# Cross attention: which batch of a tile takes the key weights' products, and which engine copies U

## The chip, the cores and the metric

The kernel runs on one core of a Trainium2 chip. The metric is the time of one execution in microseconds of device time; a run's number is a median over executions. The core has five engines with queues of their own: TensorE (PE in the profile; PEld are its weight loads), VectorE (DVE), ScalarE (ACT), GpSimd (POOL) and SyncE (SP, which issues the DMAs here). They meet only at semaphores: an instruction adds to a count when it has finished, and another engine waits until the count has reached a value.

## What is computed

A block of three parts over 2048 tokens of width 512: cross attention, self attention with a mask by pages, and a layer of eight experts of which each token uses two. Only the cross attention is touched:

```python
x = x + _L0_xattn_ref(_layernorm(x, axis=-1), ctx_512, Wq, Wkv, Wo)

def _L0_xattn_ref(x, z, Wq, Wkv, Wo):        # x: 64 x 32 x 512, z: 64 x 257 x 256
    Q = (x @ Wq.T).reshape(B, xN, 16, 32)
    KV = (z @ Wkv.T).reshape(B, zN, 2, 16, 32)
    K, V = KV[:, :, 0], KV[:, :, 1]
    attn = softmax(einsum('bqhd,bkhd->bhqk', Q, K) * 32 ** -0.5)
    O = einsum('bhqk,bkhd->bqhd', attn, V).reshape(B, xN, 512)
    return O @ Wo.T
```

There are 64 batches of 32 tokens, each with its own 257 keys.

## The kernel before

A tile is 128 tokens, that is four batches of 32 (BT = 4, j = 0 to 3, called first to fourth batch here); there are 16 tiles, taken in pairs (u = 0, 1), the first and the last pair written out and those between in a loop. The keys are never formed. Q of a tile is multiplied with the key weights once (`absorb_k`, the key products QK, 256 numbers for each of 16 heads and 128 tokens), and the scores of a batch are QK times the batch's z (`scores`). In the same way the weighted sum of z is taken first (`gather_z`, result U), and U of a tile's four batches is multiplied with the value weights at once (`values`). Products of 32-bit numbers are split into a high and a low half and three products (`product`, lines 52 to 54).

Each engine runs its own order for a batch s = 4i + j, written out by hand in a function `tile`:

- TensorE: the scores of s; in the first batch `turn_last` of the tile before; `gather_z` of s - 1; in the first batch `last_values`; in the third the transposition of the normalised x (`turn_x`, line 363); the transposition of the next z (`turn_z`, line 357); a step, if the batch has one; then in the first batch `values` of the tile before (line 436), in the second `project_o` of the tile before, in the third and fourth one half of `project_q` each for tile i + 2 (line 371); and last the transposition of the weights, `turn_p` (line 389).
- A step is two calls of `absorb_k` (line 381, 32 small products each pair). It needs the score banks, so it waits until all exponentials of the batch are done (a_E); ScalarE then copies two times 128x1024 numbers to QK (`qk_out`, line 528, semaphore a_QK), and `turn_p`, which uses two of the same banks, waits for that.
- ScalarE: four exponentials (line 573), in the first batch the copy of U of the tile's last batch before (`u_out`, line 549), the high half of QK for the next batch (`qk_hi`, line 535), in the third batch the copy of the turned x (`x_out`, line 518), the high half of z (line 514), the copies of a step, in the other batches `u_out`, in the first the high half of O, the high half of the transposed weights (line 541), and in the third and fourth batch half of Q (`q_out`, line 523).
- VectorE: the maxima of the scores (line 664), the reciprocal and the normalisation of the weights (line 676), the low half of QK (`qk_lo`, line 608), the low half of z (`z_lo`, line 603), and the low half of the transposed weights (line 616).

Which batch has a step, for which tile, and what it waits for comes from one function, `step_of`, which returns the slot of Q and QK, the first of the two products, the count of a_Q and the count of a_QK. Before, the second batch has the second pair of the next tile, and the fourth batch the first pair of the tile after the next. So two products of tile 1 are made before the tiles begin (AHEAD = 6), and TensorE waits for them there. U's copies count on a semaphore `a_U`, for which `gather_z` and `values` wait.

Of the kernel before, what the change touches and what calls it, by code (L numbers as in the profile page):

```python
# [84 lines left out]
def cross_attention(nc, x_in, ctx_in, Wq, Wkv, Wo, x_res, ident, vlast_dram, spare,  # L85
# [8 lines left out]
    NQ = C // P  # L94
    HD = 32
# [11 lines left out]
    with ExitStack() as ctx:  # L107
# [3 lines left out]
        def sem(name):  # L111
            return ctx.enter_context(nc.semaphore(name))
# [180 lines left out]
        pe_PL, pe_O, pe_Q, pe_OP = (sem(n) for n in ("pe_PL", "pe_O", "pe_Q", "pe_OP"))  # L293
        a_T, a_E, a_PT, a_U, a_QK, a_QKh = (sem(n) for n in ("a_T", "a_E", "a_PT", "a_U", "a_QK", "a_QKh"))
        a_X, a_Q, a_OT = (sem(n) for n in ("a_X", "a_Q", "a_OT"))
# [4 lines left out]
        s_end = BT * n_tile  # L300
        AHEAD = 6

# [8 lines left out]
        def step_of(i, u, j, more):  # L311

            if j == 1 and (more or u == 0):
                return 1 - u, 2, 2 * (i + 1) + 2, BT * i + AHEAD + 2
            if j == 3 and more:
                return u, 0, 2 * (i + 2) + 1, BT * i + AHEAD + 4
            return None

        with nc.Block() as block:
# [28 lines left out]
            def _(pe):  # L350
# [14 lines left out]

                def project_q(i, half):
                    if half == 0:
                        pe.wait_ge(a_X, i + 1)
                    for m in range(2 * half, 2 * half + 2):
                        for k in range(KC):  # L370
                            mm = pe.matmul(bank_o[:, m * P:(m + 1) * P], WqT[:, k, m * P:(m + 1) * P], xnT[:, k, :],
                                           start=(k == 0), stop=(k == KC - 1))
                    mm.then_inc(pe_Q, 1)
# [36 lines left out]
                def gather_z(s):  # L410

                    pe.wait_ge(g_Z, s + 1)
                    pe.wait_ge(v_PT, 2 * s + 2)
                    need(pe, a_U, s)
                    for k in range(KL):
                        for c in range(CH):
                            mm = product(pe, bank_u[:, k],
                                         (zn_hi[:, c, k * P:(k + 1) * P], zn_lo[:, c, k * P:(k + 1) * P]),
                                         (PT_hi[:, c, :], PT_lo[:, c, :]), c == 0, c == CH - 1)
                    mm.then_inc(pe_U, 1)  # L420
# [8 lines left out]
                def values(i):  # L429

                    pe.wait_ge(a_U, BT * i + BT)
                    for m in range(NQ):
                        for part in range(KL):
                            for hh in range(4):
                                h = 4 * m + hh
                                mm = pe.matmul(bank_o[hh * HD:(hh + 1) * HD, m * P:(m + 1) * P],
                                               WvT[:, part, h * HD:(h + 1) * HD], U[:, part, h, :], start=False,
                                               stop=(m == NQ - 1 and part == KL - 1), tile_position=(0, hh * HD))
                    mm.then_inc(pe_O, 1)
# [10 lines left out]
                project_q(0, 0)  # L450
                project_q(0, 1)
                turn_z(0, 0, 0)
# [5 lines left out]
                project_q(1, 0)  # L458
                project_q(1, 1)
                pe.wait_ge(a_QK, NQ)  # L460
                pe.wait_ge(a_Q, 4)
                absorb_k(Qp[1], 0)
                absorb_k(Qp[1], 1)
                pe.wait_ge(a_QK, AHEAD)

# [45 lines left out]
            def _(act):  # L511
# [35 lines left out]
                def u_out(s, j):  # L547
                    act.wait_ge(pe_U, s + 1)
                    act.copy(U[:, :, :, j * HD:(j + 1) * HD], bank_u[:].rearrange("p k (h q) -> p k h q", q=HD)
                             ).then_inc(a_U, 1)  # L550

# [7 lines left out]
                q_out(1, 1, (0, 1))  # L559
                qk_out(NQ, 1, 0)  # L560
                qk_out(NQ + 1, 1, 1)

                def tile(i, u, first, last, more):
                    for j in range(BT):
                        s = BT * i + j
                        some = not (first and j == 0)
                        step = step_of(i, u, j, more)
                        for m in range(NQ):
                            act.wait_ge(v_mx, 2 * s + m // 2 + 1)
                            if m == 0:  # L570
# [3 lines left out]
                                           scale=1.0, accum_out=rsum[:, m:m + 1]).then_inc(a_E, 1)  # L574
                        if j == 0 and some:
                            u_out(s - 1, BT - 1)
                        if not (last and j == BT - 1):
# [22 lines left out]
            def _(dve):  # L600
# [26 lines left out]
                def last_weights(i):  # L627
# [12 lines left out]
                                      head_mask[:].unsqueeze(1).unsqueeze(3).to_broadcast(heads), ALU.mult).then_inc(v_PR, 1)  # L640

                def ot_lo(i):
                    dve.wait_ge(a_OT, i + 1)
# [13 lines left out]
                def tile(i, u, first, last, more):  # L657
                    for j in range(BT):
# [14 lines left out]
                        if j == 0:  # L673
                            need(dve, v_PR, 4 * i)
                        dve.tensor_tensor(p_last[:, j, :], Pr[:, :, LAST], rinv[:], ALU.mult)
                        dve.tensor_tensor(Pr[:, :, 0:LAST], Pr[:, :, 0:LAST],
                                          rinv[:].unsqueeze(2).to_broadcast([P, NQ, LAST]), ALU.mult).then_inc(v_N, 1)
                        if not (last and j == BT - 1):
                            qk_lo(s + 1, u if j < BT - 1 else 1 - u, (j + 1) % BT)
                            z_lo(s + 1)  # L680
# [1568 lines left out]
```

## Time and profile before

| what | value |
|---|---|
| median of 3 runs | 1547.85 us (1547.23 to 1549.03) |
| the profiled execution's own time | 1552.86 us |
| its span, first to last instruction | 1551.1 us |
| mean granted clock of TensorE over the span | 0.974 |
| busy over the span: TensorE, VectorE, ScalarE, GpSimd | 94%, 69%, 53%, 35% |
| ScalarE's copy of U, 64 times | 1.03 us each (median) |
| ScalarE's copies to QK, 64 times | 1.02 us each (median) |

The profiled execution is 5.0 us longer than the median of the runs shown. Shares over the whole span mix three stages: the cross attention runs from about 22 to 714 us, then self attention, then the experts.

### The profile page before, as it was taken

Reading aid. Unit: us, or ns where it says so; the run is one execution under the profiler, and the core shown is the slowest. Engines: PE = TensorE matmul, PEld = TensorE weight load, DVE = VectorE, ACT = ScalarE, POOL = GpSimd, SP = SyncE. Lnnn points to the kernel's source line nnn. Section 1 sums busy time; section 2 is a strip of 40 time slices with the busy share of each in tenths; the row PEclk is TensorE's granted clock in tenths of the full one; section 3 lists DMA queues with packets and bytes.
Section 4 is the critical chain, followed back from the end, with each engine's and each line's share of the span. In section 5 each row is a group of like instructions: output and inputs, shape, how many; then the busy total and the mean of one; then the engine's idle time right before and its main releaser. Section 6 shows DMA issues by size and latency. Waiting matters only on the chain. (4 is left out here: it accounts for less than half of the span.)

```text
span 1551.1 us, 39390 instructions
## 1 busy us (share of the span) xinstructions
PE 1457.1 (94%) x14912; PEld 1295.2 (84%) x14912; DVE 1064.6 (69%) x1920; ACT 825.1 (53%) x1542; POOL 545.2 (35%) x816
## 2 busy tenths in 40 slices
PE   5799999999999999997899998679999999999997
PEld 5788888888888888885687876579999999999996
DVE  2466666666666676673567676687878878787874
ACT  3566666666666666663334342154554555555552
POOL 1122221222222222222856777343343332334332
PEclk8899999999999999997999999789999999999999
DMA  8101001001010001100010114147877778787871
GB/s 277 64 29 29 29 21 27 25 23 27 27 27 27 21 27 27 29 8 1 16 42 31 37 37 152 57 154 266 278 271 265 267 234 292 251 273 246 291 242 41
DMA packets 130733, 174.10 MB, mean 112 GB/s; under 512 B 16953, under 2 KB 89337, under 8 KB 130626
## 3 DMA queue, kind: packets, MB, share of 16 engines
q1 hardware_dynamic: 120242, 145.56, 28.9%
q0 software_dynamic: 10384, 27.05, 4.8%
q8 instruction: 74, 1.21, 0.3%
q14 instruction: 33, 0.27, 0.1%
HBM read 157.18 MB, written 19.06 MB: 114 GB/s over the span
## 5 line engine op out<-in xcount | busy, mean ns | idle before, releaser
L2046 DVE TENSOR_TENSOR lo<-raw,hi 128x1024 fp32r<-128x1024 f32 x207 | 246.1, 1220 | 7.8 <-ACT hi L1982 6.6
L52 PE MATMUL mo_bank<-xT_hi,hi 128*128 128x256 f32 x768 | 216.6, 282 | 3.2 <-DVE xT_lo L2055 2.8
L54 PE MATMUL mo_bank<-xT_lo,hi 128*128 128x256 f32 x768 | 215.5, 281 | 0.0
L53 PE MATMUL mo_bank<-xT_hi,lo 128*128 128x256 f32 x768 | 215.3, 280 | 0.0
L1982 ACT CAST hi<-raw 128x1024 fp32r<-128x1024 f32 x207 | 208.3, 1049 | 4.9 <-DMA raw<-in_L_ffn_W_dram 2.7
L573 ACT ACTIVATE Pr<-xa_s,nmax 128x257 f32<-128x257 f32 x256 | 119.0, 472 | 130.5 <-DVE nmax L664 130.4
L2002 ACT ACTIVATE sl<-mo_bank 128x256 f32<-128x256 f32 x117 | 44.9, 384 | 247.6 <-PE mo_bank L54 244.7
L52 PE MATMUL xa_s<-zT_hi,QK_hi 128*128 128x258 f32 x512 | 153.6, 300 | 4.0 <-ACT QK L528 2.0
L616 DVE TENSOR_TENSOR PT_lo<-xa_s,PT_hi 128x512 fp32r<-128x512 f32 x128 | 82.4, 685 | 105.9 <-ACT PT_hi L541 105.8
L52 PEld LDWEIGHTS mo_bank<-xT_hi,hi 128*128 128x128 f32 x768 | 145.2, 189 | 9.8 <-issue 5.6
L53 PEld LDWEIGHTS mo_bank<-xT_hi,lo 128*128 128x128 f32 x768 | 145.1, 189 | 3.2
L54 PE MATMUL xa_s<-zT_lo,QK_hi 128*128 128x258 f32 x512 | 146.2, 286 | 0.0
L53 PE MATMUL xa_s<-zT_hi,QK_lo 128*128 128x258 f32 x512 | 145.3, 284 | 0.0
L54 PEld LDWEIGHTS mo_bank<-xT_lo,hi 128*128 128x128 f32 x768 | 145.2, 189 | 0.0
L2130 POOL TENSOR_TENSOR e_carrier<-count 128x1 f32<-128x1 f32 x84 | 29.9, 356 | 313.2 <-DMA of_row<-slot_val 104.9
L664 DVE TENSOR_REDUCE nmax<-xa_s 128x2 f32<-128x514 f32 x128 | 88.1, 691 | 42.6 <-PE xa_s L54 40.9
L707 POOL TENSOR_TENSOR xa_carrier<-mhalf 128x1 f32<-128x1 f32 x64 | 12.6, 197 | 291.7 <-DVE QK_lo L608 287.2
L52 PE MATMUL xa_u<-PT_hi,zn_hi 128*128 128x512 f32 x256 | 103.2, 403 | 0.0
L52 PEld LDWEIGHTS xa_s<-zT_hi,QK_hi 128*128 128x128 f32 x512 | 98.0, 191 | 6.0 <-DVE zT_lo L603 2.8
L53 PE MATMUL xa_u<-PT_hi,zn_lo 128*128 128x512 f32 x256 | 101.9, 398 | 0.0
L54 PE MATMUL xa_u<-PT_lo,zn_hi 128*128 128x512 f32 x256 | 101.8, 398 | 0.0
L52 PE MATMUL mo_bank<-hi,a_hi 128*128 128x512 f32 x234 | 95.8, 409 | 5.3 <-DVE a_lo L2111 5.2
(302 smaller groups left out, 3925.5 us busy)
## 6 DMA issues: line engine op xcount, KB each, us to landing
raw<-in_L_ffn_W_dram SPq DMA_DIRECT2D x207, 512.0 KB
raw<-in_ctx_dram SPq DMA_DIRECT2D x64, 256.0 KB, 2.6
out_dram<-x_res SPq DMA_DIRECT2D x16, 256.0 KB
xs<-xn SPq DMA_DIRECT2D x16, 256.0 KB
x_res<-in_x_dram SPq DMA_DIRECT2D x1, 3840.0 KB, 18.9
VL<-v_last_rows SPq DMA_DIRECT2D x128, 2.0 KB, 1.5
raw_o<-in_L_xattn_Wo_dram SPq DMA_DIRECT2D x1, 1024.0 KB, 5.7
raw_q<-in_L_xattn_Wq_dram SPq DMA_DIRECT2D x1, 1024.0 KB, 8.8
```

Source lines behind the costliest of these rows:

```text
L52: pe.matmul(out, lh, rh, start=start, stop=False)
L53: pe.matmul(out, ll, rh, start=False, stop=False)
L54: return pe.matmul(out, lh, rl, start=False, stop=stop)
L573: act.activation(Pr[:, m, 0:NK], bank_s[:, m, 0:NK], ACT.Exp, bias=nmax[:, m:m + 1], scale=1.0, accum_out=rsum[:, m:m + 1]).then_inc(a_E, 1)
L616: dve.tensor_tensor(PT_lo[:, c, :], bank_pt[c], PT_hi[:, c, :].bitcast(F32), ALU.subtract).then_inc(v_PT, 1)
L664: dve.tensor_reduce(nmax[:, 2 * h:2 * h + 2], bank_s[:, 2 * h:2 * h + 2, 0:NK], AX_X, ALU.max, negate=True).then_inc(v_mx, 1)
L707: pool.tensor_tensor(carrier[:], mhalf[:], mhalf[:], ALU.add)
L1982: aW.done(act.copy(hi, raw), f"p{c}{q}")
L2002: aM.done(act.activation(sl[:, j % 2, :], bank_hg[j % 2][:, 0:ROWS], ACT.Silu), f"{pos}s{j}")
L2046: vW.done(dve.tensor_tensor(lo, raw, hi.bitcast(F32), ALU.subtract), f"p{c}{q}")
L2130: pool.tensor_tensor(carrier[:], count[:, 0:1], count[:, 0:1], ALU.add).then_inc(carried, 1)
```

## The change

Both pairs of the next tile's key products are made in the tile: the first pair in the first batch, the second in the third batch, instead of in the fourth batch of the tile two before and the second of the tile before. So nothing of tile 1 is made ahead of the tiles any more, and both pairs of tile 15 are made in tile 14. `project_q` waits for the copy of the turned x in both halves, and in the second half also for the copy of the first half of Q. The copy of U of a tile's last batch, which is made in the next tile's first batch, goes from ScalarE (behind the exponentials) to VectorE (behind the normalisation of the weights, ahead of `qk_lo`). The semaphore `a_U` is renamed `U_out`, since two engines count on it. The copy of U behind the last tile stays on ScalarE.

```diff
-            if j == 1 and (more or u == 0):
-                return 1 - u, 2, 2 * (i + 1) + 2, BT * i + AHEAD + 2
-            if j == 3 and more:
-                return u, 0, 2 * (i + 2) + 1, BT * i + AHEAD + 4
+            if j % 2 == 0 and (more or u == 0):
+                return 1 - u, j, 2 * (i + 1) + 2, BT * i + NQ + j + 2
             return None
...
-                def project_q(i, half):
-                    if half == 0:
-                        pe.wait_ge(a_X, i + 1)
+                def project_q(i, half, wait_first=True):
+                    pe.wait_ge(a_X, i + 1)
+                    if half == 1 and wait_first:
+                        pe.wait_ge(a_Q, 2 * i + 1)
...
                 pe.wait_ge(a_QK, NQ)
-                pe.wait_ge(a_Q, 4)
-                absorb_k(Qp[1], 0)
-                absorb_k(Qp[1], 1)
-                pe.wait_ge(a_QK, AHEAD)
...
                 q_out(1, 1, (0, 1))
-                qk_out(NQ, 1, 0)
-                qk_out(NQ + 1, 1, 1)
...
-                        if j == 0 and some:
-                            u_out(s - 1, BT - 1)
...
+                def u_out(s, j):
+                    dve.wait_ge(pe_U, s + 1)
+                    dve.tensor_copy(U[:, :, :, j * HD:(j + 1) * HD], bank_u[:].rearrange("p k (h q) -> p k h q", q=HD)
+                                    ).then_inc(U_out, 1)
...
                         dve.tensor_tensor(Pr[:, :, 0:LAST], Pr[:, :, 0:LAST],
                                           rinv[:].unsqueeze(2).to_broadcast([P, NQ, LAST]), ALU.mult).then_inc(v_N, 1)
+                        if j == 0 and not first:
+                            u_out(s - 1, BT - 1)
                         if not (last and j == BT - 1):
                             qk_lo(s + 1, u if j < BT - 1 else 1 - u, (j + 1) % BT)
                             z_lo(s + 1)
```

## Rows read from the trace of the kernel before

**Rows 1.** Busy time per engine, one tile: stretch, its length, engines, PEclk, DMA share, GB/s

```profile
307.00:348.00 41.00, 40.50 (x372) 35.92 (x371) 27.48 (x50) 27.41 (x60) 9.90 (x21) 1.00 0.09 26
```

**Rows 2.** Waits of TensorE's weight loads, 90 to 700 us: total, times, longest

```profile
PEld xa_o L436 <- ACT U L549: 6.5, 15, 0.4
PEld xa_o L371 <- ACT xg L518: 6.2, 13, 0.5
...
PEld xa_s L389 <- ACT QK L528: 3.4, 13, 0.3
```

**Rows 3.** Timeline, a first batch: start, duration, engine, line, operation, idle before

```profile
341.56 1.22 DVE L676 TENSOR_TENSOR Pr<-Pr,rinv 128x1024 f32<-128x1024 f32 x1
...
342.60 0.60 PE L357 MATMUL xa_z<-ident,raw 128*128 128x128 f32 x4
...
343.40 1.95 PE L436 MATMUL xa_o<-U,WvT 128*32 128x128 f32 x64 [0.20 <-ACT U L549]
...
345.29 1.09 PE L389 MATMUL xa_s<-ident,Pr 128*128 128x128 f32 x8
...
346.21 0.39 PE L52 MATMUL xa_s<-zT_hi,QK_hi 128*128 128x258 f32 x1
```

**Rows 4.** Timeline, a second batch

```profile
310.69 0.60 PE L357 MATMUL xa_z<-ident,raw 128*128 128x128 f32 x4
...
312.32 0.50 PE L52 MATMUL xa_o<-WoT_hi,OT_hi 128*128 128x512 f32 x1
...
316.02 0.37 PE L52 MATMUL xa_s<-zT_hi,QK_hi 128*128 128x258 f32 x1
```

**Rows 5.** Timeline, a third batch

```profile
321.81 0.60 PE L363 MATMUL xa_o<-ident,xg 128*128 128x128 f32 x4
...
322.25 0.60 PE L357 MATMUL xa_z<-ident,raw 128*128 128x128 f32 x4
...
323.09 2.05 PE L371 MATMUL xa_o<-xg,WqT 128*128 128x128 f32 x16 [0.24 <-ACT xg L518]
...
325.77 0.36 PE L52 MATMUL xa_s<-zT_hi,QK_hi 128*128 128x258 f32 x1
```

**Rows 6.** Timeline, a fourth batch

```profile
331.54 0.60 PE L357 MATMUL xa_z<-ident,raw 128*128 128x128 f32 x4
...
332.07 1.17 PE L381 MATMUL xa_s<-raw,Wk 32*128 32x128 f32 x32
...
333.18 2.05 PE L371 MATMUL xa_o<-xg,WqT 128*128 128x128 f32 x16
...
336.14 0.36 PE L52 MATMUL xa_s<-zT_hi,QK_hi 128*128 128x258 f32 x1
```

**Rows 7.** Timeline, the beginning and tile 0

```profile
41.33 0.28 PE L371 MATMUL xa_o<-xg,WqT 128*128 128x128 f32 x1
...
45.65 0.39 PE L52 MATMUL xa_s<-zT_hi,QK_hi 128*128 128x258 f32 x1 [2.04 <-ACT QK L528]
...
51.89 0.20 ACT L573 ACTIVATION_READ_ACCUMULATOR Pr<-xa_s,nmax 128x1 f32 x1
...
55.43 0.58 PE L52 MATMUL xa_s<-zT_hi,QK_hi 128*128 128x258 f32 x1
...
61.84 0.60 PE L357 MATMUL xa_z<-ident,raw 128*128 128x128 f32 x4
...
66.49 0.37 PE L52 MATMUL xa_s<-zT_hi,QK_hi 128*128 128x258 f32 x1
```

**Rows 8.** Timeline, third batch of tile 14

```profile
652.35 0.60 PE L357 MATMUL xa_z<-ident,raw 128*128 128x128 f32 x4
...
654.83 0.39 PE L52 MATMUL xa_s<-zT_hi,QK_hi 128*128 128x258 f32 x1 [0.64 <-DVE zT_lo L603]
```

**Rows 9.** VectorE's groups by line over the span: busy, mean ns, idle before

```profile
L603 DVE TENSOR_TENSOR zT_lo<-xa_z,zT_hi 128x512 fp32r<-128x512 f32 x64 | 43.9, 686 | 2.9 <-ACT zT_hi L514 2.9
```

**Rows 10.** Busy time per engine, first scores of tile 0, columns as in rows 1

```profile
45.65:50.20 4.55, 4.55 (x25) 4.55 (x26) 0.69 (x1) 1.02 (x4) 0.00 (x0) 0.62 0.00 0
```

More of the change, by code:

```diff
@@ L293, in cross_attention @@
         pe_PL, pe_O, pe_Q, pe_OP = (sem(n) for n in ("pe_PL", "pe_O", "pe_Q", "pe_OP"))
-        a_T, a_E, a_PT, a_U, a_QK, a_QKh = (sem(n) for n in ("a_T", "a_E", "a_PT", "a_U", "a_QK", "a_QKh"))
+        a_T, a_E, a_PT, a_QK, a_QKh, U_out = (sem(n) for n in ("a_T", "a_E", "a_PT", "a_QK", "a_QKh", "U_out"))
         a_X, a_Q, a_OT = (sem(n) for n in ("a_X", "a_Q", "a_OT"))
@@ L300, in cross_attention @@
         s_end = BT * n_tile
-        AHEAD = 6
         def by_pair(eng, tile):
@@ L413, in gather_z @@
                     pe.wait_ge(v_PT, 2 * s + 2)
-                    need(pe, a_U, s)
+                    need(pe, U_out, s)
                     for k in range(KL):
@@ L429, in values @@
                 def values(i):
-                    pe.wait_ge(a_U, BT * i + BT)
+                    pe.wait_ge(U_out, BT * i + BT)
                     for m in range(NQ):
@@ L450, in _ @@
                 project_q(0, 0)
-                project_q(0, 1)
+                project_q(0, 1, False)
                 turn_z(0, 0, 0)
@@ L458, in _ @@
                 project_q(1, 0)
-                project_q(1, 1)
+                project_q(1, 1, False)
                 pe.wait_ge(a_QK, NQ)
-                pe.wait_ge(a_Q, 4)
-                absorb_k(Qp[1], 0)
-                absorb_k(Qp[1], 1)
-                pe.wait_ge(a_QK, AHEAD)
                 def tile(i, u, first, last, more):
@@ L549, in u_out @@
                     act.copy(U[:, :, :, j * HD:(j + 1) * HD], bank_u[:].rearrange("p k (h q) -> p k h q", q=HD)
-                             ).then_inc(a_U, 1)
+                             ).then_inc(U_out, 1)
                 x_out(0)
@@ L565, in tile @@
                         s = BT * i + j
-                        some = not (first and j == 0)
                         step = step_of(i, u, j, more)
@@ L640, in last_weights @@
                                       head_mask[:].unsqueeze(1).unsqueeze(3).to_broadcast(heads), ALU.mult).then_inc(v_PR, 1)
+                def u_out(s, j):
+                    dve.wait_ge(pe_U, s + 1)
+                    dve.tensor_copy(U[:, :, :, j * HD:(j + 1) * HD], bank_u[:].rearrange("p k (h q) -> p k h q", q=HD)
+                                    ).then_inc(U_out, 1)
                 def ot_lo(i):
```

## The prediction

> **What bounds the kernel now.** I first read the busy time per engine over one tile of the middle of the cross attention: in 41.00 us TensorE is busy for 40.50 us at a granted clock of 1.00, while VectorE and ScalarE are busy for about 27.4 us each [rows 1]. So in this stage the time is TensorE's, and a change is worth what it takes out of TensorE's order or puts into it. Then I read whom TensorE waited for from 90 to 700 us [rows 2]: 6.5 us in 15 waits for ScalarE's copy of U, 6.2 us in 13 waits for the copy of the turned x, 3.4 us in 13 waits for the copies of the key products QK. All three are waits that the change moves. Last I read the timeline of one tile, batch by batch [rows 3 to 6], and the two ends of the stage [rows 7, 8], because the change is not symmetric there. DMA is no part of it: the tile moves its data at a DMA share of 0.09 [rows 1].
>
> I measure a batch by one stretch: from the first transposition of the next z (call it T) to the first score product of the next batch (S). What lies ahead of T, scores and gathering of z, the change leaves alone. T to S is now
>
> - first batch: 346.21 - 342.60 = 3.61 us [rows 3],
> - second: 316.02 - 310.69 = 5.33 us [rows 4],
> - third: 325.77 - 322.25 = 3.52 us [rows 5],
> - fourth: 336.14 - 331.54 = 4.60 us [rows 6],
>
> in sum 17.06 us of the tile.
>
> **Key products moved to the first and third batch.** TensorE's instructions stay the same in number: two absorptions per step, 32 small products, two steps a tile. ScalarE's copies of them move along; no DMA moves.
>
> The fourth batch loses its step. T is followed by 0.44 us of transposes, read from two runs of four behind each other (322.25 - 321.81) [rows 5]. Then comes the projection, and from its start to S without a wait for QK the third batch shows 325.77 - 323.09 = 2.68 us [rows 5]. New: 0.44 + 2.68 = 3.12 us, 1.48 less. Its projection newly waits for ScalarE's copy of the first half of Q; that copy stands right behind the third batch's copies of the transposed weights, so it is done a batch earlier, and I cost the wait at nothing.
>
> The second batch loses its step too. Its output projection starts 312.32 - 310.69 = 1.63 us after T [rows 4], without the step after 0.44: 1.19 less, 4.14 us new. Can the chain follow? At a batch without any step (the third of tile 14) S waits for the low half of z, and T to S is 654.83 - 652.35 = 2.48 us [rows 8]. That is the floor of the chain, and 3.12 and 4.14 lie above it, so TensorE's work still sets both.
>
> The third batch gets a step. Now it has T, projection, transposition of the weights; new it has T, step, projection, transposition, which is what the fourth batch does now, its wait for the QK copies included: 4.60 us, 1.08 more. The wait for the turned x (6.2 us in 13) goes, since the step lies in front of the projection: 1.64 us from T to the projection [rows 6] against 0.84 now [rows 5]. ScalarE has one copy more to do here than in the fourth batch, but it does it before the step's products have ended.
>
> The first batch gets a step as well, ahead of the values' products. These take 1.95 us [rows 3], the projection in the fourth batch 2.05 [rows 6], so the same form fits: 4.60 us, 0.99 more. Queued behind TensorE's wait for QK is the transposition of the weights; on ScalarE the copies (ahead of the copies of O and of the weights) end about when the values' products end, so these two follow with the gap to TensorE that they have now. If the QK wait cost nothing here, 0.15 would be saved; if the values begin late, up to 0.44, today's wait, is added.
>
> Sum for a tile: 0.99 - 1.19 + 1.08 - 1.48 = -0.60 us, with bounds of -0.75 and -0.16. Thirteen tiles (1 to 13) have this form: -7.8 us, from -9.8 to -2.1.
>
> **U copied by VectorE.** VectorE copies after it has normalised the weights. That operation starts at 341.56 and takes 1.22 us [rows 3], so it ends 0.18 us after T. The values start 1.64 us after T, so a copy of up to 1.46 us costs nothing. The trace has no copy of 128x1024 from this memory on VectorE. The nearest rows are the same number of elements in SBUF, 1.22 us [rows 3], and twice the 128x512 subtraction that reads PSUM, 2 x 0.686 = 1.37 us [rows 9]. I take 1.25 as an estimate, nearer to the row with as many elements in one operation; both ends are under 1.46. Behind it on VectorE stand the low halves of QK and of z (1.22 and 0.686 us), which then end about 3.4 us after T, and S is due at 4.60. ScalarE is rid of about as long a copy and reaches its own QK copy earlier. The cover is the step; where there is none, in tile 15, the values now start 0.80 us after T (343.40 - 342.60, [rows 3], since tile 15 has the same first batch) and will start at 0.18 + 1.25 = 1.43 plus a little: 0.6 us more, bounds 0.6 and 0.8.
>
> The Trainium skill (Perfetto Trace Analysis, Optimizing Scalar/DVE Operations) speaks against this move: it gives VectorE a fixed cost of about 125 ns at an access to PSUM and ScalarE about 51 ns. With the 0.96 GHz that the Trainium skill gives (VectorE: DVE Perf Modes, Specifications), an estimate from these two pages for the copy is 1024/0.96 + 125 = 1.19 us; by that the last tile would lose 0.06 us less, and nothing else of the sum would change. No run here shows such a copy yet.
>
> **The ends.** In the beginning, TensorE now waits before its first scores for Q, absorbs two pairs of tile 1 and waits for their copies: scores start at 45.65, while the projection before them has its last product at 41.33 [rows 7]. New they start at about 41.6: 4.05 us earlier. Tile 0 then takes the step in its first batch, with little to cover it. There the exponentials end at 52.09, 6.44 us after the first scores, and from a step's start to S the fourth batch shows 336.14 - 332.07 = 4.07 us [rows 6]: 10.5 us in place of 55.43 - 45.65 = 9.78 [rows 7], 0.7 more. The clock is open here: the scores ran at a granted clock of 0.62 [rows 10] after a stretch in which TensorE mostly waited. If they run at 1.00, 4.55 us of them become 4.55 x 0.62 = 2.8, and 0.7 more becomes 1.0 less; if the transposition of the weights (1.09 us, [rows 3]) falls to half clock, it takes twice that, and it is 1.8 more. In the second batch the step goes and there is no output projection yet: T to S was 66.49 - 61.84 = 4.65 [rows 7] and falls to the floor of 2.48, 2.17 less. Third and fourth batch as in every tile: +1.08 and -1.48. Tile 0: -4.05 + 0.7 - 2.17 + 1.08 - 1.48 = -5.9 us, from -7.6 to -4.8.
>
> In tile 14 the first and second batch give +0.99 - 1.19. Its third batch gets a step with no projection to cover the copies: 4.60 in place of 2.48, +2.12; its fourth had no step. Tile 14: +1.9. Tile 15: +0.6.
>
> **Sum.** -7.8 - 5.9 + 1.9 + 0.6 = -11.2 us; with all bounds together from -15.5 (-9.8 - 7.6 + 1.9) to -4.2 (-2.1 - 4.8 + 1.9 + 0.8). The profiled span of 1551.1 us becomes 1539.9, its own execution 1552.9 becomes 1541.7; the median of the runs, 1547.85, lies 5.0 under that execution, and the same difference from it gives 1536.7 us.
>
> **Rivals.**
>
> *The cover runs short in the first and third batch.* If ScalarE is late with the QK copies by 0.3 us in each, a tile gains nothing and only the ends count: -5.9 + 1.9 + 0.6 = -3.4, 1544.5 us. For it: the wait for these copies exists already in the fourth batch, 0.26 us at a time (3.4 us in 13) [rows 2], so there is no reserve. Against it: that wait is inside the 4.60 us that I used.
>
> *It ends slower: VectorE is late with U.* The place is the first batch, where everything behind the values waits. Each microsecond of the copy over 1.46 costs 14 us over tiles 1 to 14 (and one more in tile 15). To be slower by 0.2%, 3.1 us, the forecast must lose 14.3 us: the copy would have to take about 2.4 us. Against it are both nearest rows, 1.22 and 1.37; for it only that the copy's output is in strips of 32 elements, which no VectorE row out of PSUM has. At 2.4 us: 1551 us and above.
>
> *What is saved is given back later.* If the next stage waited for something that is not tied to the end of this one, the time would stay at 1547.85. Against it: TensorE is first after the end of this stage in a chain of its own work, and DMA is nearly idle here.
>
> **How the numbers follow.** A change of 0.2%, 3.1 us, is what a measurement of this kernel can tell from none. I give the forecast 0.70, the short cover 0.15, given back 0.07, slower 0.08. The short cover lies just beyond the border, so two thirds of it count as faster: faster 0.80, same 0.12, slower 0.08. The forecast's own range is from 1532.3 to 1543.6. The range reaches over the short cover to 1546 and, since the clock of the beginning is the least known term, to 1531 below.
>
> **What would show it.** In the profile after: a period of a tile shorter by 0.6 us; no wait of the projection for the turned x; the values starting behind the step with no wait for U; VectorE's copy of U 1.2 to 1.4 us long; the wait of the transposition for QK twice a tile, 0.3 us each; scores of the first batch beginning near 41.6 us; the third batch of tile 14 longer by 2.1. I am wrong if the QK waits of first and third batch are 0.6 us or more, or if S waits for the low half of z in a middle tile.

## The result and the profile after

The changed kernel takes 1571.36 us in the median (four runs, 1565.95 to 1574.53) against 1547.54 of the kernel before on the same chip: a ratio of 1.0153, interval 1.0119 to 1.0188. It is slower by 1.5%, where 0.7% faster was forecast. The profiled span grew from 1551.1 to 1572.8 us.

First the places that the forecast spoke of. A middle tile of the kernel after, from one first score product to the same one of the next tile, busy time per engine with the columns of [rows 1]:

```profile
307.63:348.10 40.47, 40.24 (x376) 36.14 (x374) 28.90 (x51) 26.49 (x60) 9.83 (x22) 1.00 0.10 28
```

This tile is shorter by 0.85 us than the 41.32 that thirteen tiles of before have in the mean. The timeline of its four batches, to be held against [rows 3 to 6]:

```profile
302.97 1.22 DVE L633 COPY U<-xa_u 128x1024 f32<-128x1024 f32 x1
...
303.03 0.60 PE L354 MATMUL xa_z<-ident,raw 128*128 128x128 f32 x4
303.56 1.17 PE L379 MATMUL xa_s<-raw,Wk 32*128 32x128 f32 x32
304.66 1.96 PE L434 MATMUL xa_o<-U,WvT 128*32 128x128 f32 x64
306.78 1.09 PE L387 MATMUL xa_s<-ident,Pr 128*128 128x128 f32 x8 [0.16 <-ACT QK L522]
307.63 0.36 PE L52 MATMUL xa_s<-zT_hi,QK_hi 128*128 128x258 f32 x1
...
313.40 0.60 PE L354 MATMUL xa_z<-ident,raw 128*128 128x128 f32 x4
...
317.44 0.36 PE L52 MATMUL xa_s<-zT_hi,QK_hi 128*128 128x258 f32 x1
...
323.64 0.60 PE L354 MATMUL xa_z<-ident,raw 128*128 128x128 f32 x4
...
328.24 0.36 PE L52 MATMUL xa_s<-zT_hi,QK_hi 128*128 128x258 f32 x1
...
334.02 0.60 PE L354 MATMUL xa_z<-ident,raw 128*128 128x128 f32 x4
...
337.03 0.36 PE L52 MATMUL xa_s<-zT_hi,QK_hi 128*128 128x258 f32 x1
```

T to S is 4.60, 4.04, 4.60 and 3.01 us; forecast were 4.60, 4.14, 4.60 and 3.12. VectorE's copy of U takes 1.22 us (1.25 was taken), begins 0.06 us ahead of T, and the values start behind the step with no wait. So in a tile everything came as forecast, a little better. The time must have gone somewhere else, and the waits of TensorE's weight loads say where (after, 90 to 720 us: total, times, longest, as in [rows 2]):

```profile
PEld xa_s L54 <- issue: 17.3, 5, 3.8
PEld xa_s L387 <- ACT QK L522: 11.8, 28, 2.3
PEld xa_s L52 <- issue: 10.3, 5, 2.2
...
PEld xa_o L434 <- DVE U L633: 0.8, 1, 0.8
```

The wait for the turned x is gone and that for U is down from fifteen to one; the wait for QK comes twice a tile, 0.43 us in the first batch and 0.25 in the third of the tile above, and 2.3 us once, in tile 14:

```profile
306.78 0.85 PEld L387 LDWEIGHTS xa_s<-ident,Pr 128*128 128x128 f32 x8 [0.43 <-ACT QK L522]
...
327.39 0.85 PEld L387 LDWEIGHTS xa_s<-ident,Pr 128*128 128x128 f32 x8 [0.25 <-ACT QK L522]
...
673.93 1.02 PEld L387 LDWEIGHTS xa_s<-ident,Pr 128*128 128x128 f32 x8 [2.29 <-ACT QK L522]
```

But there are two new rows whose releaser is "issue", which means that the engine waited for nothing that the profile shows: five times each, 27.6 us together. One of the five places in TensorE's timeline (after):

```profile
200.65 1.04 PE L387 MATMUL xa_s<-ident,Pr 128*128 128x128 f32 x8
203.66 0.36 PE L52 MATMUL xa_s<-zT_hi,QK_hi 128*128 128x258 f32 x1 [1.98 <-issue]
207.20 0.38 PE L53 MATMUL xa_s<-zT_hi,QK_lo 128*128 128x258 f32 x1 [3.18 <-issue]
207.37 0.42 PE L54 MATMUL xa_s<-zT_lo,QK_hi 128*128 128x258 f32 x1
```

and the busy time per engine in the stretches around it:

```profile
190.00:201.00 11.00, 10.94 (x84) 10.15 (x83) 5.84 (x10) 8.41 (x17) 2.54 (x6) 1.00 0.09 28
201.00:207.20 6.20, 1.04 (x9) 0.74 (x7) 1.95 (x6) 1.36 (x3) 1.34 (x2) 0.98 0.16 45
207.20:210.20 3.00, 3.00 (x15) 3.00 (x15) 0.44 (x1) 0.00 (x0) 0.00 (x0) 0.50 0.02 5
210.20:216.00 5.80, 5.80 (x52) 4.95 (x54) 4.70 (x9) 3.54 (x10) 0.31 (x2) 0.99 0.00 0
```

TensorE stands idle for 1.98 us, runs one score product, stands idle for 3.18 us, and then 15 score products run for 3.00 us at a granted clock of 0.50, the 1.2 GHz level, before the clock is 0.99 again. Nothing on the other engines holds it up: they too have little to do. The place is the first scores of tiles 4, 6, 8, 10 and 12. The kernel's loop goes over two tiles, so these are its five returns from the end of its body to the begin. The starts of the values in three tiles show what one return costs (after; a row holds only those of the 64 products that fall into the short window):

```profile
304.66 0.41 PE L434 MATMUL xa_o<-U,WvT 128*32 128x128 f32 x5
...
345.13 0.64 PE L434 MATMUL xa_o<-U,WvT 128*32 128x128 f32 x16
...
393.15 0.41 PE L434 MATMUL xa_o<-U,WvT 128*32 128x128 f32 x6
```

From tile 6 to 7, inside the body, it is 40.47 us; from 7 to 8, over a return, 48.03 (48.02 by the rounded rows). Over the five returns the periods are 47.37, 47.76, 48.03, 48.17 and 48.30: 239.63 - 5 x 40.47 = 37.3 us that the kernel before does not have, whose periods are 41.31 to 41.37 throughout.

One more view answers to this: the DMA queues from 130 to 640 us (packets, MB, share), before and after.

```profile
q8 instruction: 7, 0.11, 0.1%
```

```profile
q8 instruction: 51, 0.84, 0.7%
```

Queue q8, which carries instructions, moved 44 packets more in these 510 us, and 45 more in the whole profile (119 against 74), nine for each return; they are of 0.84 MB / 51 = 16 KB each.

So the account of the difference, from the traces: the values in tile 1 start 7.42 us earlier (87.99 against 95.41); thirteen periods save 13 x 0.85 = 11.0; the returns cost 37.3; tile 14 costs 3.0 more (40.78 against 37.78) and the last tile 1.0 (37.78 against 36.78); behind the stage 1.2 are gained. Sum: -7.4 - 11.0 + 37.3 + 3.0 + 1.0 - 1.2 = +21.7, the difference of the spans.

### The profile page after: what moved, and what is told of

Its sections match the earlier page's. It is cut to its first block and busy times, and to the rows that moved or that the text cites. A ratio compares the mean times of both kernels' runs of the same rounds, so it can differ in the third digit from the quotient of the medians.

```text
span 1572.8 us, 39406 instructions
## 1 busy us (share of the span) xinstructions
PE 1457.5 (93%) x14912; PEld 1301.5 (83%) x14912; DVE 1082.3 (69%) x1935; ACT 811.9 (52%) x1527; POOL 542.3 (34%) x816
## 5 line engine op out<-in xcount | busy, mean ns | idle before, releaser
L52 PE MATMUL xa_s<-zT_hi,QK_hi 128*128 128x258 f32 x512 | 156.8, 306 | 11.2 <-issue 9.3
L53 PE MATMUL xa_s<-zT_hi,QK_lo 128*128 128x258 f32 x512 | 149.3, 292 | 16.8 <-issue 16.8
L54 PE MATMUL xa_s<-zT_lo,QK_hi 128*128 128x258 f32 x512 | 149.9, 293 | 0.0
L54 PEld LDWEIGHTS xa_s<-zT_lo,QK_hi 128*128 128x128 f32 x512 | 102.3, 200 | 17.3 <-issue 17.3
L52 PEld LDWEIGHTS xa_s<-zT_hi,QK_hi 128*128 128x128 f32 x512 | 102.3, 200 | 13.0 <-issue 10.3
L53 PEld LDWEIGHTS xa_s<-zT_hi,QK_lo 128*128 128x128 f32 x512 | 103.1, 201 | 0.0
```

What stands on the lines that cost most here:

```text
L52: pe.matmul(out, lh, rh, start=start, stop=False)
L53: pe.matmul(out, ll, rh, start=False, stop=False)
L54: return pe.matmul(out, lh, rl, start=False, stop=stop)
```

## The experiments

**The theories.** *Theory 1*: TensorE's code arrives in pieces of 16 KB, 256 instructions, and a number of them is held. The changed kernel issues two absorptions fewer ahead of its loop, 32 products in the trace with a weight load each, 64 instructions; with one wait more, its loop begins 63 places earlier in the code than before. Where a loop's code lies over one piece more, its first piece is no longer there at the return. *Theory 2*: the moved steps or VectorE's copy cause the idle stretches. A loop can be moved in the code without touching its content: satisfied waits in TensorE's part of the setup, before any data has arrived there, where they cost little as long as they are few (two of the waits below make one instruction: with N = 15 the 30 waits are 15 more records on TensorE's queue):

```diff
                     for n, (load, blocks, _dst, width) in enumerate(jobs):
+                        for _ in range(2 * N if n == 1 else 0):
+                            pe.wait_ge(loaded[3], 16)
                         pe.wait_ge(loaded[load], 16)
```

**A correction ahead of the texts on record.** The expectations of the first six kernels count the loop's body as 1244 or 1246 instructions, and so five or six pieces. That was too low: a product of two fp32 operands that is written once runs as two (the values of a tile are 32 in the code and x64 in the timeline above). With these counted twice the body has 1564 instructions before and 1566 after, of which 1488 are the matmuls and weight loads of two tiles. The traces bear this out: from one branch at the body's end to the next TensorE's queue has 1564 records in the kernel before and 1566 in the changed one, 744 of them matmuls and 744 weight loads in both. The packets of q8 keep step with that count: in the kernel before seven of them start from 126.5 to 207.9 us, 13.57 us apart in the mean, and at 1564 instructions in a pass of 82.65 us (178.09 to 260.74) that is one for 257 instructions. The numbers of pieces that are told apart are seven and eight, not five and six. The place at which the loop begins in a piece, 250 of 256 for the changed kernel, comes from where the idle stretches fall: between its first score products, some six instructions behind its begin. All other places below are counted from that one; with the two kernels' begins 63 apart, the stalls in the table below, and their absence, allow 249 to 253 for it. The table at the end of this section has every kernel by the right count.

**First set: the changed kernel moved by 15, by 2 and by 45, the kernel before by 15.** N is 15, 2, 45 and 15.

> The changed kernel with 15 more instructions on TensorE's queue, all of them waits that are satisfied when they come, put where TensorE waits 3.9 us for the output weights in the setup, long ahead of the loop. Nothing else differs. Theory 1 (place of the loop in the code): TensorE's code comes in pieces of 256 instructions; the loop of the cross attention has 1246 and now begins 5 instructions ahead of the end of a piece, so it touches six; with 15 more it begins 10 behind a boundary and ends 24 ahead of the next (10 + 1246 = 1256 of 1280), so it touches five, as the loop of the kernel before did. The idle of TensorE at the loop's return (10.3 + 17.3 us in the profile after) goes, with the half clock behind it, and the gain that was forecast shows: about 1537 us, 0.7% under the kernel before. Theory 2 (the new waits of the projection or the moved steps make TensorE idle): nothing changes, about 1571 us.

Measured: 1539.53 us, ratio 0.9919 (0.9888 to 0.995). The idle stretches are gone, 74 instruction packets as before, all periods up to tile 14 are 40.47 to 40.61. TensorE's longest waits in this kernel (90 to 720 us):

```profile
PEld xa_s L389 <- ACT QK L524: 11.3, 27, 2.3
PEld sa_bank L921 <- ACT sa_xn L1099: 4.8, 1, 4.8
PEld xa_s L381 <- issue: 4.5, 27, 0.2
```

Fifteen instructions that do nothing take the changed kernel's ratio from 1.0153 to 0.9919. That alone ends Theory 2 as the cause of the loss.

> As the run with 15 more instructions, but with 2. Theory 1: the loop begins 3 ahead of the boundary in place of 5 and still touches six pieces: about 1571 us, with the same idle at the loop's return. If what helps in the run with 15 is only that some instructions were added in the setup, and not where the loop comes to lie, this run is fast too, about 1537 us.

Measured: 1572.63 us, ratio 1.0136 (1.0114 to 1.0158), 119 packets, idle stretches at all five returns. That two more instructions change nothing was to be: the loop then begins at 252.

> As the run with 15 more instructions, but with 45. Theory 1: the loop begins 40 behind a boundary and ends at 40 + 1246 = 1286 of 1280, so it touches six pieces again, the last with 6 instructions only: the return to a piece that is no longer held costs 2 us at each of the loop's returns, and what follows depends on how soon the next piece comes: 1545 to 1571 us. Theory 3 (only a beginning right ahead of a boundary costs, not the number of pieces): as with 15, about 1537 us.

Measured: 1535.79 us, ratio 0.991 (0.9882 to 0.9939), 74 packets, no idle stretch. Theory 1 as then counted foresaw stalls here and missed; by the right count this loop ends at 1605, in seven pieces.

> The kernel before with the same 15 waits. Its loop of 1244 instructions begins 26 behind a boundary by theory 1 and ends at 1270 of 1280; with 15 more it ends at 1285, six pieces. Theory 1: slower by 8 to 33 us, though not one instruction of the loop has changed. Theories 2 and 3: no change, 1547 us.

Measured: 1553.27 us, ratio 1.0013 (0.9992 to 1.0033), 74 packets, no idle stretch. The cost that Theory 1 foresaw here did not come: a miss, and it was the count of instructions that had made the expectation.

**Second set: far moves and the two parts alone.** The kernel before is moved by 225, the changed one by 150. So many waits need a second place (the first job, with a semaphore that is already there), and they cost time of their own: first scores at 57.70 us for 225 in the kernel before (45.65 without), at 50.98 for 150 in the changed one (41.17).

```diff
+                        for _ in range(2 * N0 if n == 0 else 0):
+                            pe.wait_ge(nc.const_ready, 4)
+                        for _ in range(2 * N1 if n == 1 else 0):
+                            pe.wait_ge(loaded[3], 16)
                         pe.wait_ge(loaded[load], 16)
```

> The kernel before with 225 more satisfied waits on TensorE's queue in the setup, where it waits for its first weights (6.0 and 3.9 us). Its loop then begins 6 instructions ahead of a boundary of 256, as that of the changed kernel does, and nothing of the loop has changed. Theory 1 as mended by the runs so far (the loop costs when the code of its first piece is no longer held at the return): 5 returns with 2.1 + 3.3 us of idle and about 3 us at half clock behind each, so 25 to 35 us slower than the kernel before, about 1580 us, and 119 packets of instructions in place of 74. Theory 2 (it is the changed order of the work that makes TensorE idle there): no slower than the 1 to 3 us that the waits themselves may cost.

Measured: 1563.68 us, ratio 1.0106 (1.0067 to 1.0146), 75 packets, periods of 41.3 throughout. No return stalls. Against 1548.18 of the kernel before beside it that is 15.5 us more, of which the late beginning is 57.70 - 45.65 = 12.05; the rest lies inside the interval (10.4 to 22.6 us). Again a miss of the wrong count: by the right one this loop lies from place 26 to 1590, in seven pieces.

> The changed kernel with 150 more satisfied waits in the setup. The loop begins some 145 behind a boundary and ends 111 into its sixth piece. Theory 1, mended: pieces are fetched ahead, so it counts how far the loop runs into a sixth piece before it returns; with 45 more it ran 5 to 6 instructions into it and cost nothing, with 150 it runs 111 into it, the first piece is gone at the return, and each of 5 returns costs about 2 us; the next piece comes in time, since 111 instructions lie ahead of it: about 1549 us and 119 packets. Theory 3 (only a beginning right ahead of a boundary costs): as with 15, about 1537 us and 74 packets.

Measured: 1542.27 us, ratio 0.9958 (0.994 to 0.9975), 75 packets, no idle stretch: a miss of the same count, since this loop ends at 1710, in seven pieces too. The next two kernels take the change apart. In the first the changed kernel, moved by 15, has U of a tile's last batch copied by ScalarE as before; in the second the kernel before has only that copy moved to VectorE.

```diff
 # ScalarE, changed kernel
+                        if j == 0 and not first:
+                            u_out(s - 1, BT - 1)
 # VectorE, changed kernel
-                        if j == 0 and not first:
-                            u_out(s - 1, BT - 1)
```

> The changed kernel with the 15 waits, but U of a tile's last batch copied by ScalarE again, behind the exponentials: the moved steps alone. The forecast's terms: the copy of 1.03 us stands ahead of the high half of QK, the high half of z and the two QK copies on ScalarE, so these end about 0.4 us later and the transposition of the weights waits longer in the first batch: about 6 us slower than the run with 15, about 1544 us. Rival: ScalarE has room before the step's products end, no difference: 1538 us.

Measured: 1542.93 us, ratio 0.9956 (0.993 to 0.9982), a period of 40.81 against 40.47 with VectorE's copy: beside the moved steps that copy is worth 0.34 us a tile. The waits for QK grow from 11.3 to 15.3 us:

```profile
PEld xa_s L389 <- ACT QK L524: 15.3, 27, 2.3
```

> The kernel before with U of a tile's last batch copied by VectorE, its steps left where they were: the other part alone, with the loop of TensorE in its old place. By the forecast's terms the values wait for VectorE in 15 tiles, 0.6 us more than they wait now: about 9 us slower, 1557 us. Rival (the copy is hidden all the same): 1548 us.

Measured: 1557.49 us, ratio 1.0065 (1.004 to 1.0091). Alone the copy loses, for no step covers it: TensorE now waits 1.1 us for U in a first batch instead of 0.43.

```profile
PEld xa_o L436 <- DVE U L642: 16.5, 15, 1.4
```

**Third set: number of pieces or place of the begin?** So far a second reading was left, called Theory 3 below: that a loop stalls when it begins right ahead of a piece's border, however long it is. Four kernels tell the two apart, and show whether the stall needs the change at all. The moves use both places of the far moves above, N0 + N1 = 193, 240 and 226.

> The kernel before with 193 satisfied waits in TensorE's setup code, which moves its loop over two tiles (1564 instructions with each fp32 product counted as the two that the trace shows) to place 250 of a piece of 256, where the changed kernel's loop begins. Control: the same kernel moved by 225. Theory 1 (a loop whose code touches eight pieces is fetched anew at each return): 250 + 1564 = 1814, eight pieces; about 119 instruction packets in place of 74 or 75, TensorE idle without a releaser behind each return, some 7 us at each of five, so about 1563 + 36 = 1597 us, with no part of the change in it. Theory 2 (the moved key products or VectorE's copy cost the time by themselves): as the control, about 1562 us, 75 packets.

Measured: 1580.31 us, ratio 1.0186 (1.015 to 1.0222), 93 packets. The kernel before, with no part of the change in it, stalls at the return, but at two of the five only (periods of 49.29 and 49.28, the others 41.3). Its weight loads' waits:

```profile
PEld xa_s L52 <- issue: 6.3, 2, 3.2
PEld xa_s L54 <- issue: 5.5, 2, 3.0
```

Theory 1 has the place and the packets right (18 more than the control, nine for each stall), and the number of stalls wrong.

```diff
                     for m in range(NQ):
-                        mm = product(pe, bank_o[:], (OT_hi[:, m, :], OT_lo[:, m, :]),
-                                     (WoT_hi[:, m, :], WoT_lo[:, m, :]), m == 0, m == NQ - 1)
+                        mm = pe.matmul(bank_o[:], OT_hi[:, m, :], WoT_hi[:, m, :], start=m == 0, stop=m == NQ - 1)
```

> The changed kernel, its output projection of the cross attention with the product of the two high halves alone (the two products with a low half are left out, 8 of 12 a tile), and 16 waits that keep the loop's begin at place 250. The loop has 1534 instructions and ends at 1784, inside the seventh piece. Theory 1 (number of pieces): no idle stretch at the returns, 74 packets, and 1537 less at most 15 x 1.7 us of left out work: 1512 to 1537 us. Theory 3 (a loop that begins right ahead of a piece's border stalls there whatever its length): stalls and some 119 packets remain, 1546 to 1571 us.

Measured: 1511.85 us, 74 packets, periods of 39.12 to 39.22 up to tile 14, no idle stretch, though the loop begins where the changed kernel's does. That is Theory 1, and Theory 3 is out. (The ratio to before, 0.9755, holds the work that is left out.)

> The changed kernel moved by 240 instructions: loop from place 234 to 1800, eight instructions into the eighth piece. Theory 1: stalls at the five returns and some 119 packets, about 36 us over the next kernel. Theory 3: the border lies 22 instructions behind the loop's begin and is fetched in time, no stall, as the next kernel.

Measured: 1590.72 us, ratio 1.026 (1.0231 to 1.0289), 120 packets. The waits of its weight loads:

```profile
PEld xa_s L53 <- issue: 11.3, 5, 2.6
PEld xa_s L52 <- issue: 11.0, 5, 2.3
```

> The changed kernel moved by 226 instructions: loop from place 220 to 1786, six instructions short of the eighth piece. Theory 1: no stalls, 75 packets, tile periods of 40.5 us throughout; the waits themselves delay the beginning as in the two kernels moved far, so 1545 to 1552 us. Theory 3: the same time as the kernel moved by 240.

Measured: 1553.30 us, ratio 1.002 (1.0004 to 1.0035), 75 packets, periods of 40.47 to 40.61, no idle stretch. Fourteen instructions of do-nothing code are the only difference between these two, and they are worth 1590.72 - 1553.30 = 37.4 us; in the profiles 32.2 us of it lie in the five periods over the returns (234.55 - 5 x 40.48). TensorE's longest wait in the kernel moved by 226 is the old one, and none at the loop's begin is left:

```profile
PEld xa_s L392 <- ACT QK L527: 11.8, 28, 2.3
```

The one loop ends 8 instructions behind the seventh piece's end, the other 6 ahead of it.

**Fourth set: the kernel before at the same edge.** Open was why it had stalled at two returns only. N0 + N1 is 177 and 200.

> The kernel before, its loop at place 234 to 1798, six instructions into the eighth piece (moved by 193 it ended 22 into it and stalled at two of five returns). Theory 1 (the piece behind the loop's last is fetched ahead while the last runs, and puts the first out): stalls at all five returns, some 119 packets, as the changed kernel with eight instructions in the eighth piece: 1561 + 5 x 8 = 1601 us. Rival (the changed steps are needed for a stall at each return, and the kernel before alone stalls at some only): two of five again, some 93 packets, about 1578 us.

Measured: 1570.44 us, ratio 1.013 (1.0089 to 1.0172); in the profile one return of five stalls (period 47.66), 84 packets. The four runs lie at 1565.6, 1566.1, 1574.8 and 1575.9, in two pairs some 9 us apart. One stall more in two of them would fit, but that isn't shown: the seven runs of the kernel before beside them spread over 12.3 us with no stall in its profile. Theory 1 in its strict form, a stall at each return and 1601 us, missed; its rival, some returns only, came nearer.

> The kernel before moved by 200, seven instructions more than the one that stalled at two returns: its loop begins just behind a piece's border, place 1 to 1565, and touches seven pieces. Theory 1: no stall, 74 or 75 packets, about 1561 us. Rival (the many waits ahead of the loop cost the time): as moved by 193, about 1580 us.

Measured: 1562.92 us, ratio 1.0082 (1.0051 to 1.0113), 75 packets, periods of 41.30 to 41.38 up to tile 14, no idle stretch: seven instructions more than the kernel with two stalls, and by the ratios (1.0186 against 1.0082) 16 us less.

All kernels by the right count (place of the loop's begin and end, pieces touched; packets of the whole profile; stalls at five returns in the profile; the kernel before took 1547.5 to 1551.4 us beside them in the five sets of runs):

| kernel | loop from, to | pieces | packets | stalls | median us |
|---|---|---|---|---|---|
| before | 57, 1621 | 7 | 74 | 0 | 1547.85 |
| changed | 250, 1816 | 8 | 119 | 5 | 1571.36 |
| changed, moved 2 | 252, 1818 | 8 | 119 | 5 | 1572.63 |
| changed, moved 240 | 234, 1800 | 8 | 120 | 5 | 1590.72 |
| changed, moved 226 | 220, 1786 | 7 | 75 | 0 | 1553.30 |
| changed, moved 15 | 9, 1575 | 7 | 74 | 0 | 1539.53 |
| changed, moved 45 | 39, 1605 | 7 | 74 | 0 | 1535.79 |
| changed, moved 150 | 144, 1710 | 7 | 75 | 0 | 1542.27 |
| changed, short loop | 250, 1784 | 7 | 74 | 0 | 1511.85 |
| before, moved 15 | 72, 1636 | 7 | 74 | 0 | 1553.27 |
| before, moved 225 | 26, 1590 | 7 | 75 | 0 | 1563.68 |
| before, moved 200 | 1, 1565 | 7 | 75 | 0 | 1562.92 |
| before, moved 193 | 250, 1814 | 8 | 93 | 2 | 1580.31 |
| before, moved 177 | 234, 1798 | 8 | 84 | 1 | 1570.44 |

The two kernels that take the change apart lie in seven pieces as well and have 74 packets. No loop in seven pieces stalled; each one in eight did, the changed kernel's at every return.

**What tells a return that stalls from one that doesn't.** The traces have the start of every packet of q8 and of TensorE's branch at the body's end. In the five profiles with eight pieces 18 returns stalled. At each of them one packet starts 0.3 to 2.5 us ahead of the branch, a second about 1 us behind it and a third 4 to 5.6 us behind it; nine come in all, the loop's eight pieces and one more. At the seven returns of the same profiles without a stall there is none from 6 us ahead of the branch to 9 us behind it. In the kernel before moved by 193 (222 to 225 us, then 225 to 232, around its first stall; 302 to 395 us, with the return at 314.9, shows none):

```profile
q8 instruction: 1, 0.02, 2.0%
...
q8 instruction: 2, 0.03, 1.9%
```

By the count of nine, the packet ahead of the branch is the piece behind the loop's last. So a return stalls when that piece has been asked for before the branch goes back, and the loop's first two pieces then come one after the other while TensorE stands idle.

## Why the prediction was wrong

**The step that failed.** It is the sentence under the moved key products, "TensorE's instructions stay the same in number", together with the part on the ends, which costs the two absorptions ahead of the first scores as time only. In number they stay the same where they run, but 64 of them leave the code ahead of the loop and come back in the last tiles behind it, and the loop moves by 63 places. No term of the sum and none of the rivals had the loop's return in it. Its price, 37.3 us in the profile, is three times the forecast gain.

**What a stall is made of.** Of the 6.9 to 7.8 us at a return the one shown has 1.98 + 3.18 = 5.16 us of idle TensorE; then 15 products run at half clock, where a full clock does one in 0.12 us (the step from one score product to the next at 210.37 to 211.21). Products overlap, so the sum goes from start to start: transposition to first score product 3.01 us where a batch inside the body has 0.85 (306.78 to 307.63), first to second product 3.54 where 0.20 is usual (210.17 to 210.37), and 15 steps from 207.20 to 210.37 in 3.17 us where 1.8 would do. That is 2.16 + 3.34 + 1.37 = 6.87 us, this return's whole price (47.37 - 40.47 = 6.90). What the clock did is in the rows: it was 1.00 up to the return, TensorE then was busy for 1.04 of 6.20 us, and the granted clock fell to 0.50 when work came back.

**The page that bears on it.** The Trainium skill (Runtime: NRT & Kernel Launch, Instruction fetch mechanics) says that TensorE has room for 128 KiB of instructions, filled in order in blocks of 16 KiB or 256 instructions with the next one fetched while the current one runs, and that a taken branch to a block outside the window that is held waits for its transfer. The 16 KB packets agree, and so does the packet ahead of the branch at each stall. 128 KiB would be eight such blocks: with one block fetched ahead, a loop over eight can have pushed out its first when it returns, and a loop over seven cannot. That is an estimate from the page, and the edge between 1786 and 1798 agrees with it (seven blocks end at 1792). The same section speaks of a window of two blocks only; here the trace of before differs, for its loop of seven pieces returned five times with 7 instruction packets from 130 to 640 us and no idle stretch, and the measurement decides.

**What held, by its own steps.** A middle tile: -0.85 us where -0.60 was forecast and -0.75 was the bound; 0.21 of the difference are the second and fourth batch (4.04 and 3.01 where 4.14 and 3.12 stood), both because what is left in them ran a little tighter than the rows from which they were put together. The copy of U: 1.22 us, no wait in a middle tile, and the last tile's T to S grew from 3.60 to 3.93, 0.3 where 0.6 was forecast. The waits for QK: twice a tile, 0.43 and 0.25 us, where 0.3 each was forecast. The first scores: 41.17 us where 41.6 was forecast. The beginning gained more than forecast: tile 1's first scores start at 79.89 against 88.15, 8.3 us earlier, 5.9 forecast. The clock is most of that, as the range had left room for: from S to T, which the change leaves alone, tile 0 takes 22.09 us in its four batches against 24.40, 2.31 less; its first and third stretch ran at a granted clock of 0.62 and 0.78 before and run at 1.00 now, its second at 0.89 before and 0.81 now. The beginning of the changed kernel, to be held against [rows 7]:

```profile
41.17 0.36 PE L52 MATMUL xa_s<-zT_hi,QK_hi 128*128 128x258 f32 x1
...
49.42 1.54 PE L387 MATMUL xa_s<-ident,Pr 128*128 128x128 f32 x8 [2.10 <-ACT QK L522]
50.62 0.56 PE L52 MATMUL xa_s<-zT_hi,QK_hi 128*128 128x258 f32 x1
...
57.57 0.60 PE L354 MATMUL xa_z<-ident,raw 128*128 128x128 f32 x4
...
60.06 0.39 PE L52 MATMUL xa_s<-zT_hi,QK_hi 128*128 128x258 f32 x1 [0.64 <-DVE zT_lo L592]
```

The scores now run at full clock, as their 0.36 us and the 2.97 us from 41.17 to T at 44.14 show (4.50 us before, 45.65 to 50.15), but the step in the first batch finds no cover and TensorE waits 2.10 us for QK: from first scores to S 9.45 us, 0.3 less than before where 0.7 more was forecast. In the second batch T to S is 2.49 us, the floor of 2.48 that was taken from tile 14. In the third batch of tile 14 T to S is 4.88 us in place of 2.48, 2.4 more where 2.1 was forecast, with the same wait of 2.10 us. Behind it the granted clock is 0.79 from 675.01 to 682.09 us, and S to T takes 7.08 us there against 5.80 before; the forecast had no term for that:

```profile
670.13 0.60 PE L354 MATMUL xa_z<-ident,raw 128*128 128x128 f32 x4
670.66 1.17 PE L379 MATMUL xa_s<-raw,Wk 32*128 32x128 f32 x32
673.94 1.42 PE L387 MATMUL xa_s<-ident,Pr 128*128 128x128 f32 x8 [2.10 <-ACT QK L522]
675.01 0.56 PE L52 MATMUL xa_s<-zT_hi,QK_hi 128*128 128x258 f32 x1
```

**The forecast without the stall.** The changed kernel moved by 15 or 45 places has ratios of 0.9919 and 0.991: 12.5 and 13.9 us of 1547.85, so 1535.3 and 1533.9 us, where 1536.7 was forecast with a range of its own from 1532.3 to 1543.6. The mechanism of the change was right; the sum lacked a term that isn't in the order of work at all. The rivals did not come: the cover in the first and third batch was enough, VectorE was not late, and nothing was given back later.

**What "would show it" could not show.** Each point of that list came true in the middle tiles, the sizes roughly, and neither sign of being wrong appeared there; a wait for QK over 0.6 us came in tile 0 and tile 14 alone, 2.3 us each, where the steps have no cover. The time was outside the range all the same. The list looked at the tiles' inside only. A period measured over a return would have belonged in it.

**What stays open.** Why the piece behind the last is asked for ahead of the branch at each of the 15 returns of the changed kernel's three profiles in eight pieces, and in the kernel before only at three of ten; behind that kernel's last branch, which doesn't go back, it came 1.1 and 1.4 us late. Both end as far into the eighth piece (8 and 6 places, or 24 and 22). They differ in what TensorE waits for at the body's end: the kernel before waits for QK ahead of its last transposition, the changed one does not. That this decides whether the piece is asked for in time is a guess; no kernel with such a wait at the changed body's end was run.

**The faster version.** The changed kernel with 45 (or 15) instructions of padding ahead of its loop beats both kernels: 1535.79 us, 0.9% under before.

## What to carry to other kernels

A loop has a place in the code, and an edit ahead of it moves it: before costing an edit to a kernel whose engine is the bound, count that engine's instructions in the loop's body (fp32 products twice) and ahead of it, and see whether the body's pieces of 256 are near what is held, seven here. In the profile the sign is "issue" as releaser at the first instructions of the body, once for each return, and a count of instruction packets that grows with the number of passes. When a change is slower though each tile is faster, compare periods inside the body with those over the return before looking for a dependency.

## What the runs showed of the hardware

- A loop of TensorE in seven pieces of 16 KB is held: the kernel before has no packet of q8 from 209 to 630 us, over five returns. In eight pieces each stall came with nine packets (119 against 74 for five), so the whole body is fetched again, and one piece more; at each of 18 stalls that one started 0.3 to 2.5 us ahead of the branch, and at seven returns without it there was no stall.
- Such a return costs 5.6 to 8.0 us (5.6: 46.12 - 40.48, moved by 240; 8.0: 49.29 - 41.32, the kernel before moved by 193): 3.4 us idle (2.85 + 0.51, moved by 177) to 5.9 us (3.00 + 2.92, moved by 193), and a stretch at a granted clock of 0.50 around and behind it (3.00 us in the changed kernel).
- Whether an eight-piece loop stalls can differ from return to return of one execution (two of five in the kernel before moved by 193, one of five moved by 177).
- 225 instructions of satisfied waits of TensorE ahead of the first data put its first scores off by 12.05 us, about 54 ns each; 15 of them cost nothing that can be measured (1.0013, 0.9992 to 1.0033).
- VectorE copied 128x1024 fp32 elements out of PSUM in 1.22 us, the same as its operation of that size in SBUF [rows 3].
